# The product buffer of the gather passes: from SBUF into three PSUM banks

## The reference

```python
def gcn_conv(x, src, dst, W, b, n_nodes):      # block 4, twice; block 1 is much the same
    norm = dinv[src] * dinv[dst]
    h = x @ W
    msg = h[src] * norm[:, None]
    return jax.ops.segment_sum(msg, dst, num_segments=n_nodes) + b

def _edgeconv(x, src, dst, tw, tb, pw, pb):     # block 3, four layers
    phi = x @ pw.T + pb
    msg = (x[src] - x[dst]) @ tw.T + tb + phi[dst]
    agg = jax.ops.segment_max(msg, dst, num_segments=x.shape[0])
    return jnp.where(jnp.isneginf(agg), 0, agg)

# block 2: filter weights from the edge attributes, times h[src], summed per destination
```

## Time and profile before

| | us |
|---|---|
| three timed runs, median | 10542.4 |
| lowest and highest of them | 10541.9 and 10545.94 |
| profiled execution, span from first to last instruction | 10630.0 |
| POOL busy | 8032.4 (76%) |
| DVE busy | 4419.4 (42%) |
| PE busy | 1639.5 (15%) |
| ACT busy | 543.8 (5%) |

### The profile page before, as it was taken

One profiled execution on the slowest core, in us unless ns is written; L12 is line 12 of the kernel. 1 busy time (PEld: TensorE's weight loads), 2 busy tenths in 40 slices (PEclk: granted clock), 3 DMA queues, 4 the chain that ended last, 5 costly groups with the idle time before them and its releaser, 6 DMA issues. The chain is left out here.

```text
span 10630.0 us, 49732 instructions
## 1 busy us (share of the span) xinstructions
PE 1639.5 (15%) x9025; PEld 1437.8 (14%) x9025; DVE 4419.4 (42%) x9272; ACT 543.8 (5%) x1417; POOL 8032.4 (76%) x7137
## 2 busy tenths in 40 slices
PE   2000048888860000100001000100001000010000
PEld 1000047777750000100001000100001000010000
DVE  4444434444443444344443444334444444444444
ACT  2000021111130000000000000000001000000000
POOL 4777768888847777677776777777777777777777
PEclk7555567777775555555555555555555555555555
DMA  5444435555532333333333333323333333333333
GB/s 190 142 142 142 145 88 77 77 74 76 77 86 91 95 95 95 99 95 95 95 97 97 95 95 95 101 93 95 95 95 98 96 95 95 95 100 95 95 95 104
DMA packets 467313, 1064.01 MB, mean 100 GB/s; under 512 B 156534, under 2 KB 276192, under 8 KB 412586
## 3 DMA queue, kind: packets, MB, share of 16 engines
q0 software_dynamic: 320736, 464.07, 19.8%
q1 hardware_dynamic: 143480, 597.45, 15.5%
q10 hardware_dynamic: 2940, 1.00, 0.0%
HBM read 517.80 MB, written 552.72 MB: 101 GB/s over the span
## 5 line engine op out<-in xcount | busy, mean ns | idle before, releaser
L991 POOL DMA_INDIRECT WORK<-table,S x5824 | 6249.0, 1073 | 2037.5 <-issue 1772.7
L1045 DVE TENSOR_TENSOR Z<-WORK,RESET 128x512 f32<-128x512 f32 x612 | 423.5, 692 | 2615.7 <-DMA WORK<-table,S 2601.8
L1210 POOL DMA_INDIRECT acc<-TOT,stage x832 | 1300.8, 1564 | 276.0 <-issue 207.6
L1090 PE MATMUL bank<-ident,WORK 128*128 128x128 f32 x7 | 3.3, 474 | 8069.6 <-DVE WORK L1074 8069.6
L1045 DVE TENSOR_TENSOR Z<-WORK,KEEP 128x512 f32<-128x512 f32 x459 | 317.6, 692 | 1958.9 <-DMA WORK<-table,S 1948.5
L1090 PEld LDWEIGHTS bank<-ident,WORK 128*128 128x128 f32 x7 | 1.3, 183 | 8071.1 <-DVE WORK L1074 8071.1
L1048 DVE TENSOR_TENSOR WORK<-WORK,Z 128x512 f32<-128x512 f32 x1071 | 741.0, 692 | 36.5
L1064 DVE TENSOR_TENSOR WORK<-WORK,Z 128x1536 f32<-128x1536 f32 (+2 forms) x448 | 633.8, 1431 | 12.4
L1059 DVE TENSOR_TENSOR Z<-WORK,S 128x1536 f32<-128x1536 f32 (+2 forms) x448 | 633.6, 1431 | 12.3
L1415 DVE SCALAR_TENSOR_TENSOR BASE<-bank,WEIGHT,BASE 128x128 f32<-128x128 f32 x832 | 234.2, 344 | 839.8 <-PE bank L1285 772.3
L1053 DVE SCALAR_TENSOR_TENSOR WORK<-WORK,S 128x128 f32<-128x128 f32 x1428 | 502.5, 352 | 50.9
(11 more groups left out here) (247 smaller groups left out, 2663.4 us busy)
## 6 DMA issues: line engine op xcount, KB each, us to landing
run_rows<-WORK SPq DMA_DIRECT2D x357, 1024.0 KB, 4.1
WORK<-table,S POOLq DMA_INDIRECT x5824
fill_rows<-BASE SPq DMA_DIRECT2D x52, 1024.0 KB, 6.8
WORK<-fill_rows SPq DMA_DIRECT2D x104, 512.0 KB
table<-TF SPq DMA_DIRECT2D x56, 384.0 KB
WORK<-carry_rows SPq DMA_DIRECT2D x49, 384.0 KB
acc<-TOT,stage POOLq DMA_INDIRECT x832
acc<-Z SPq DMA_DIRECT2D x12, 1024.0 KB
```

The source lines that it names most:

```text
L991: pool.indirect_dma_start(RING_T[:, b * WIDE + k, :], None, table, table_row(table, INDEX[:, t:t + 1]))\
L1045: step(dve.tensor_tensor(TMP[:, 0:groups, 0, :], rows[:, :, j - 1, :], mask(keep[:, :, j], groups, 0), op0))
L1210: pool.indirect_dma_start(acc_dram[a], bass.IndirectOffsetOnAxis(stage[:, h, j % HALF:j % HALF + 1].bitcast(u32), 0), TOT[:, j // QUAD % 2 ...
```

## The change

`TMP` becomes a view of banks 5, 6 and 7, with the index j (0 to 2) outermost, so that one j of all four groups fills one bank. To have three banks beside each other in one view, the four PSUM tensors become one of eight banks. The lines that use `TMP` (1045, 1048, 1059, 1064) keep their text. So lines 1045 and 1059 now read two SBUF tiles and write PSUM, and lines 1048 and 1064 read one SBUF tile and PSUM and write SBUF. `bank(i)` names the same banks. No instruction is added, removed or moved on any engine. Line numbers after line 226 are smaller by one up to line 229 and the same from there on.

```diff
-        TMP = Z[:, 0:3 * GROUPS * F].rearrange("p (g j f) -> p g j f", g=GROUPS, j=3)
         RING_T = WORK[:, :].rearrange("p (t f) -> p t f", f=F)
 
-        banks = [ctx.enter_context(nc.psum_tensor(f"bank{i}", [P, 1024], f32)) for i in range(4)]
+        banks = ctx.enter_context(nc.psum_tensor("bank", [P, 4096], f32))
+        TMP = banks[:, 5 * 512:8 * 512].rearrange("p (j g f) -> p g j f", j=3, g=GROUPS)
...
         def bank(i, n=1):
-            return banks[i // 2][:, i % 2 * 512:(i % 2 + n) * 512]
+            return banks[:, i * 512:(i + n) * 512]
```

## The result

| | before | after |
|---|---|---|
| timed runs, median, us | 10542.15 | 10236.65 |
| lowest and highest | 10541.65 and 10545.94 | 10233.24 and 10243.07 |
| profiled span, us | 10630.0 | 10237.1 |

The ratio is 0.9711, 95% interval 0.9697 to 0.9724: 305.5 us faster, where 329 were forecast. The predicted time was 10213 us.

The account below looks back on a forecast made before the run. POOL's gathers were taken to set the pace, losing 751 us to holds by DVE instructions; 422 us would remain, a gain of 329 from 10542.4 to 10213 us. Own range 10088 to 10453; 8 in 10: 9950 to 10400.

Parts of the forecast that it names:

- POOL's pace, and 751 us over the median: Line 991's gathers run at POOL's pace; their time over the 944 ns median sums to 751 us.
- What holds a read: two SBUF inputs: A gather's want 0.13 us after its start waits for the end of DVE tensor-tensors with both inputs in SBUF.
- Rival 3: The hold belongs to the tensor-tensor wherever its second input is; nothing changes, 10542 us; chance 0.04.
- rival 2: With their output in PSUM, L1045 and L1059 hold nothing either, so no gather is held: 9791 us; chance 0.06.
- L1053 holds none.: In the chunk, the gather that reads in the fourth L1053 takes 0.95 us, so L1053 delays no gather.
- The gain is not the share of the two lines: Gathers freed from L1048 and L1064 run on; a whole chunk loses 1.48 us in L1059 instead of 2.08.
- The write term w: Change per DVE instruction writing PSUM (L1045, L1059): taken as 0, bounds -157 to +157 ns; ten ns are 13 to 14 us.
- the sum: Loss over all chunks: 266 x 1.48 + 91 x 0.31 = 422 us instead of 751, a gain of 329 us.
- DVE pays nothing: After a chunk's 9.5 us DVE waits 12.57 us for the next rows, so longer instructions stay hidden except through the read.
- The gain in us carried to the timed runs: The 329 us gain is taken off the timed median of 10542.4 us, giving 10213 us.
- Rival 1: Longer L1048 makes L1059 start too late for the read: 186 us lost, gain 565, time 9977 us; chance 0.06.
- Rival 4: DVE writes PSUM at a lower rate; at half rate L1059 lasts 3.36 us, time about 11480 us; chance 0.03.

Follow-up runs that it names:

- e4_masks: The changed kernel with the masks of lines 1045 and 1059 in PSUM as well, by two copies per pass: 9799.2 us, 0.9308 of the kernel before.
- e5_masks_only: Masks in PSUM as in e4_masks, but the product buffer TMP back in SBUF: 10413.4 us, 0.9876 of the kernel before.
- e1_pairs: The changed kernel with the buffer of lines 1059 and 1064 back in SBUF, that of 1045 and 1048 in PSUM: 10428.6 us, 0.9905 of before.
- e3_later: The changed kernel plus a 128x64 DVE memset ahead of L1059 in every chunk, not waited for: 10239.8 us, 0.9727 of the kernel before.

## Why the prediction was right, point by point

- **POOL's pace, and 751 us over the median.** Right. e4_masks takes 742 of the 751 us away and the time falls by 729, without touching POOL's instructions.
- **What holds a read: two SBUF inputs.** Right, and shown from both sides: L1048 and L1064 became free with the second input in PSUM, L1045 and L1059 with the mask there (e4_masks), and the hold came back on L1048 and L1064 when the buffer alone went back (e5_masks_only). For L1045 this is counted over the traces: it held 26 reads in the changed kernel and none of 43 in e4_masks. Rival 3 (the instruction holds wherever its second input is) and rival 2 (nothing holds once the output is in PSUM) are both out: the gain came, and in the profile after, L1059 writes PSUM and holds. What a gather wants 0.13 us after its start, no run shows; "read" is a name for it.
- **"L1053 holds none."** Wrong, at a price of 0.8 us in the profile after, where it holds 8 of 357 reads, and of 8.6 us in e4_masks. The gather on which this rests reads 0.05 us into the fourth L1053, well ahead of the 0.19 from which the earlier trace rows show a hold; the reads that L1053 does hold lie 0.23 us or more into it.
- **The gain is not the share of the two lines.** Right. A freed gather runs into the next hold; the whole chunk loses 1.52 us in one place, for 1.48 on paper. e1_pairs shows the same by itself.
- **The write term w.** Taken as 0, it is +8 to +10 ns; and reading from PSUM gave 6 ns, not 11. So L1059 ends 3 x (8 + 5) + 10 = 49 ns later than in the sum. As an estimate, 357 x 0.049 = 17 us of the 20 by which the loss was underestimated (442 against 422) come from there. Counted over the trace, L1059 costs 437 us, 15 more than the sum; the other 5 are lost beside L1045, L1053 and line 1074, which the sum left out. These are the terms that were mis-sized.
- **DVE pays nothing.** Right: after a chunk it still waits, 11.96 us in the one shown.
- **The gain in us carried to the timed runs.** Right: 309 us in the gathers of the profiles, 305.5 in the medians. Taking the ratio of the spans would have been wrong, since the profile before had 87 us outside the gathers, by which its span stood over the median of its timed runs.
- **Rivals 1 and 4.** Rival 1 did not come of itself, since L1048 was not longer. The margin was thinner than the one chunk of the prediction said, and that it held was in part luck: there the read fell 0.28 us into L1059, but in 107 of the 266 whole chunks of the profile after it fell less than 0.22 us into it, and up to 0.17 a read is free. Rival 4 is out: L1059 writes PSUM in 1767 ns, where it wrote SBUF in 1757.

## What to carry to other kernels

Where POOL's indirect DMAs set the pace, look at the spread of one line's gathers, not at their mean: here those that ended 0.8 us behind a DVE instruction were held by it, and what mattered of that instruction was whether two of its inputs were in SBUF. Moving one input (a mask will do, as well as a product) to PSUM cost no DVE instruction more than 10 ns here, and it paid in full only when the last tensor-tensor with two SBUF inputs was gone; until then a freed gather ran on into the next one. Walk through the chunk with POOL's times and DVE's side by side before you count on a share.

## What the runs showed of the hardware that was not expected

- A DVE tensor-tensor with one input or its output in PSUM is about as fast as one with everything in SBUF: for 128x512, 692 ns with everything in SBUF (before), 686 with one input in PSUM and 700 with the output there (after), 696 with both an input and the output there (e4_masks).
- A gather's read can put off DVE too, when it falls shortly before the point from which it would be held. The second L1053 of the chunk shown after has a read 0.21 us into it and takes 0.41 us, where the median is 0.35; the one of the earlier trace rows with a read 0.05 us into it is not longer. The four take 1.57 us after and 1.51 before. In the earlier trace rows it is the L851 with a read at 0.17 that takes 1.02 us, against 0.96.

```profile
4799.63 0.41 DVE L1053 SCALAR_TENSOR_TENSOR WORK<-WORK,S 128x128 f32<-128x128 f32 x1
4799.72 0.94 POOL L991 DMA_INDIRECT WORK<-table,S  x1 [0.30 <-issue]
```

- A DVE instruction that does not wait for the memset ahead of it began 0.03 us after that memset did (e3_later). To put an instruction off, it has to wait for the one ahead of it.
